# A two-layer decoder on one core: four chains with their own buffers, new engine orders, and the experts' weights applied on GpSimd

## The reference

```
g = silu(einsum('bsd,efd->bsef', x, Wg)); u = einsum('bsd,efd->bsef', x, Wu)
out_e = einsum('bsef,edf->bsed', g * u, Wd); routed_out = einsum('bsed,bse->bsd', out_e, w_full)
```

## Time and profile before

| | |
|---|---|
| executions of the kernel | 618.33 us median of 3 (615.70, 618.33, 619.99) |
| the profiled execution | span 616.0 us from first to last instruction |
| PE busy | 523.1 us (85% of the span), 2416 instructions |
| DVE busy | 498.5 us (81%), 1133 |
| ACT busy | 428.5 us (70%), 962 |
| POOL busy | 266.5 us (43%), 418 |
| DMA | 63.59 MB, mean 103 GB/s |

### The profile page before, as it was taken

One profiled execution on the slowest core, in us unless ns is written; L12 is line 12 of the kernel. 1 busy time (PEld: TensorE's weight loads), 2 busy tenths in 40 slices (PEclk: granted clock), 3 DMA queues, 4 the chain that ended last, 5 costly groups with the idle time before them and its releaser, 6 DMA issues.

```text
span 616.0 us, 8787 instructions
## 1 busy us (share of the span) xinstructions
PE 523.1 (85%) x2416; PEld 372.7 (60%) x2416; DVE 498.5 (81%) x1133; ACT 428.5 (70%) x962; POOL 266.5 (43%) x418
## 2 busy tenths in 40 slices
PE   4956674898776899999889998899999899989856
PEld 3534453566653567767566677676776767767634
DVE  2089999998989999999986979999899996544332
ACT  2597579699968867897966986995798692332211
POOL 1088567346785522647432565564344421101110
PEclk9876587699979999999989999899999999999969
DMA  7295020382204460166005550560272047042000
GB/s 201 79 377 201 1 70 1 101 264 87 69 1 112 127 194 2 50 196 197 0 1 151 144 147 5 167 202 1 77 232 64 2 129 235 0 129 94 10 0 9
DMA packets 29823, 63.59 MB, mean 103 GB/s; under 512 B 4752, under 2 KB 8592, under 8 KB 29392
## 3 DMA queue, kind: packets, MB, share of 16 engines
q1 hardware_dynamic: 29776, 63.04, 33.3%
HBM read 61.91 MB, written 1.11 MB: 102 GB/s over the span
## 4 chain that ended last, share of the span: by engine, by line
PE 42%; DVE 26%; ACT 15%; issue 10%; POOL 3%; SPq 2%; DMA 1%; DVEq 0%; POOLq 0%; ACTq 0%
PE work L610 24%; PE work L667 9%; DVE acc L1187 5%; DVE st L1171 5%; ACT dA L962 5%; PE work L586 3%; PE h_bank L586 3%; DVE m L1136 2%; ACT L962 2%; DVE wk L1140 2%; ACT L831 2%; DVE h_tok L1089 2%; POOL dbu L548 2%; DVE du L1105 2%; DVE bst L1014 2%
## 5 line engine op out<-in xcount | busy, mean ns | idle before, releaser
L548 POOL TENSOR_TENSOR dbu<-du,b_rows 128x512 f32<-128x512 f32 x128 | 163.1, 1275 | 82.1 <-DVE st L1171 60.6
L962 ACT ACTIVATE dA<-dts,a_neg 128x127 f32<-128x127 f32 x512 | 156.9, 355 | 17.2 <-DVE st L1171 16.1
L1171 DVE TENSOR_TENSOR_SCAN st<-dA,dbu 128x512 f32<-128x512 f32 x128 | 155.1, 1214 | 6.4 <-ACT dA L962 6.1
L586 PE MATMUL h_bank<-ident,st 128*128 128x128 f32 x512 | 89.1, 305 | 41.2 <-DVE acc L1187 32.4
L610 PE MATMUL work<-stream,xsT 128*128 128x352 f32 (+1 forms) x320 | 111.1, 485 | 4.5 <-ACT xsT L831 1.9
L586 PEld LDWEIGHTS h_bank<-ident,st 128*128 128x128 f32 x512 | 66.3, 156 | 74.3 <-DVE st L1171 55.6
L1187 DVE SCALAR_TENSOR_TENSOR acc<-h_bank,c_cols,acc 128x512 f32<-128x512 f32 x128 | 92.9, 726 | 0.5 <-PE h_bank L586 0.4
L610 PEld LDWEIGHTS work<-stream,xsT 128*128 128x128 f32 x320 | 59.4, 200 | 33.8 <-issue 3.6
L493 POOL TENSOR_SCALAR var<-mv 128x1 f32<-128x1 f32 x56 | 12.7, 227 | 132.0 <-DVE mv L1015 131.1
L831 ACT ACTIVATE h_t<-work 128x384 f32<-128x384 f32 (+2 forms) x64 | 30.8, 482 | 37.6 <-PE work L586 37.5
L962 ACT ACT_TABLE_LOAD x43 | 55.2, 1283 | 0.8
(11 more groups left out here) (159 smaller groups left out, 824.4 us busy)
## 6 DMA issues: line engine op xcount, KB each, us to landing
stream<-in_stream SPq DMA_DIRECT2D x72, 352.0 KB, 3.5
stream<-in_stream SPq DMA_DIRECT2D x32, 384.0 KB, 3.7
b_rows<-b_dram SPq DMA_DIRECT2D x32, 256.0 KB, 4.4
stream<-in_stream SPq DMA_DIRECT2D x8, 360.0 KB, 3.7
stream<-in_stream SPq DMA_DIRECT2D x8, 256.0 KB, 2.7
wg<-in_wg SPq DMA_DIRECT2D x1, 1280.0 KB, 8.5
wu<-in_wu SPq DMA_DIRECT2D x1, 1280.0 KB, 11.0
wd<-in_wd SPq DMA_DIRECT2D x1, 1280.0 KB, 13.6
```

What stands on the lines that cost most here:

```text
L548: gp.tensor_tensor(tile, du[:, batch % 2, :, lo:hi], b_rows[:, b % 2, k:k + 1, :].to_broadcast([P, ET, P]), ALU.mult).then_inc(s["dbu_read ...
L586: return nc.tensor.transpose(dst, src, ident[:, :])
L962: last = A(dA[i % DA_RING][:, t, 1:P], dts[:, batch % 2, t, lo + 1:hi], ACT.Exp, scale=a_neg[:, t, k:k + 1])
L1171: V.tensor_tensor_scan(st[:, i % ST_RING].rearrange("p t l -> p (t l)"), dA[i % DA_RING].rearrange("p t l -> p (t l)"), dbu[:, i % DBU_RIN ...
```

## The change

Six things are done together.

1. The chains `0` and `1` are cut in two each: `m` (out and xat0), `f` (ffn0), `h` (hgrn), `g` (ffn1). Each has its own `r`, `xsT`, `bst`, `mv`, `var`, `rstd` and semaphores; rows 2 and 5, which hand a unit from one chain to the next, are doubled. So the second chain of a layer can be at unit u while the first is at u + 1, or later.
2. All four orders and `BANK` are new.
3. SP has an order of its own, with letters for the loads (`l`), the chunks of the stream (`c`), the store and spread of B (`b`, `r`), rows of x (`w`, `x`) and the output rows (`o`).
4. `STREAM_RING` goes from 6 to 5 and `ACC_RING` from 4 to 3.
5. For a routed chunk, POOL multiplies the experts' weights into `h_tok` once ACT has written the SiLU there, one instruction for the chunk, with the weights broadcast along each expert's columns. DVE waits for that and makes one plain product of the chunk.
6. Some waits are new: a `D` sum waits for the normalised row of the unit before, `S` waits for its readers, and so on.

The diff, cut to its core (the new strings of `ORDER` and `BANK` are shortened to PE's last lines, the start of PE's and DVE's and that of SP's):

```diff
-ACC_RING = 4
+ACC_RING = 3
-STREAM_RING = 6
+STREAM_RING = 5
...
-    layer0 = [("out", k) for k in range(6)] + [("xat0", k) for k in range(5)] + [("ffn0", k) for k in F0.steps]
-    layer1 = [("hgrn", k) for k in range(8)] + [("ffn1", k) for k in F1.steps]
+    mixer0 = [("out", k) for k in range(6)] + [("xat0", k) for k in range(5)]
...
-        "0": [(stage, u, k) for u in range(U) for stage, k in layer0],
-        "1": [(stage, u, k) for u in range(U) for stage, k in layer1],
+        "m": [(stage, u, k) for u in range(U) for stage, k in mixer0],
+        "f": [("ffn0", u, k) for u in range(U) for k in F0.steps],
+        "h": [("hgrn", u, k) for u in range(U) for k in range(8)],
+        "g": [("ffn1", u, k) for u in range(U) for k in F1.steps],
...
     "pe": [
-        "ppp0ppppss00pppassssssaaaaaaaaaaaaasssssssssssss0ssp00sss00000spppssspsppsssss0000ss0ss0000s000000s0000s0s00s0",
+        "ppppppppmsmpassssssssssasssssssssssmmsmssssmmppssmspsspppsssffsmmmmpsssffffffffffppssspsfmmmmssffsfsfffsfmmsff",
...
-        "10100s110100001s1s111s1111011s000s00s0s111100000ss00001000000000001110100a110110000111111110000111000000000001",
-        "1110000001011110011111111111111111111111111111111111",
+        "gghsmmmmsffggfhhsfffgfsfggmmmfgmggffggmmggmgfffffffffffgfgfffgggfhhhhgghghfffffgfffhhffaaaaaaaaaaaaaffffffffgg",
+        "ffgfggghhhhghhgggghhgggggggggggggggggggggppsmmmfhhhg",
...
     "dve": [
-        "saa0000111pppppppsssssssssssssssspsppppppssassaaass0s00sssssas0s0as0ss00sp00s0ss00ppppppasa000aa000sa000000000",
+        "ppppppppsssssssssssssssssspsssssssmmmmmsmsssssmmsaaamsmsmasffsffspppppppafaffasasssassfffasasmmmmmsfffaamsfffs",
...
+    "sp": [
+        "lllclllcccbcrrlbccrccbxcwccccccccrccccccccrccccwcbcccwrcccccwcccccocccrccccccccoccccccccccccccccccccocrcwccccc",
+        "ccccccccccccocwccccocccccccccccccccccccccooo",
+    ],
...
-        row1, row2, row4, row5, row6 = (sb(f"row{i}", [P, H]) for i in (1, 2, 4, 5, 6))
-        row3 = sb("row3", [P, 2, H])
+        row1, row4, row6 = (sb(f"row{i}", [P, H]) for i in (1, 4, 6))
+        row2, row3, row5 = (sb(f"row{i}", [P, 2, H]) for i in (2, 3, 5))
...
-        r = [sb(f"r{i}", [P, H]) for i in range(2)]
-        xsT = [sb(f"xsT{i}", [P, HT, P]) for i in range(2)]
+        r = [sb(f"r{i}", [P, H]) for i in range(4)]
+        xsT = [sb(f"xsT{i}", [P, HT, P]) for i in range(4)]
...
+                if stage in ("ffn0", "ffn1") and isinstance(k, str) and k[0] == "U":
+                    f, c = (F0, F1)[stage == "ffn1"], int(k[1:])
+                    if f.lo[c] < f.routed:
+
+                        lo, hi = f.experts_of(c)
+                        pool.wait_ge(wf_ready[f.lay], b + 1)
+                        pool.wait_ge(*read(f"G{f.lay}_{c}", b))
+                        h = h_tok[f.lay][:, f.lo[c]:f.hi[c]].rearrange("p (e l) -> p e l", e=hi - lo)
+                        gp.tensor_tensor(h, h, wf[f.lay][:, lo:hi, :].to_broadcast([P, hi - lo, f.width]), ALU.mult)\
+                            .then_inc(weighed[f.lay], 1)
...
                 elif k == f.sum:
-                    add_bank(f.stage, u, rows(rows_in, u), lay)
+                    if u:
+                        dve.wait_ge(*row(rows_in + 1, u - 1))
+                    add_bank(f.stage, u, rows(rows_in, u), (FFN0, FFN1)[lay])
...
                     c = int(k[1:])
-                    dve.wait_ge(*read(f"G{lay}_{c}", u))
+                    if f.lo[c] < f.routed:
+                        dve.wait_ge(weighed[lay], f.routed_chunks * u + c + 1)
+                    else:
+                        dve.wait_ge(*read(f"G{lay}_{c}", u))
                     dve.wait_ge(*full(f"U{lay}_{c}", u))
                     t = work_bank(f"U{lay}_{c}", u)
-                    for lo, hi, e in f.weighted(c):
-                        h, up = h_tok[lay][:, lo:hi], t[:, lo - f.lo[c]:hi - f.lo[c]]
-                        if e is None and lay == 0:
-                            last = V.tensor_tensor(h, h, up, ALU.mult)
-                        else:
-                            weight = pr[:, 2:3] if e is None else wf[lay][:, e:e + 1]
-                            last = V.scalar_tensor_tensor(out=h, in0=h, scalar=weight, in1=up,
-                                                          op0=ALU.mult, op1=ALU.mult)
+                    h = h_tok[lay][:, f.lo[c]:f.hi[c]]
+                    up = t[:, 0:f.hi[c] - f.lo[c]]
+                    if f.lo[c] < f.routed or lay == 0:
+                        last = V.tensor_tensor(h, h, up, ALU.mult)
+                    else:
+                        last = V.scalar_tensor_tensor(out=h, in0=h, scalar=pr[:, 2:3], in1=up,
+                                                      op0=ALU.mult, op1=ALU.mult)
                     release(last, f"U{lay}_{c}", u)
```

More of the change, by code:

```diff
@@ L49, in __init__ @@
         self.chunks = len(self.lo)
+        self.routed_chunks = sum(a < self.routed for a in self.lo)
         self.k_tiles = -(-self.total // P)
@@ L86, in chains @@
         "a": [("adj", b, k) for b in range(B) for k in range(ADJ_STEPS)],
-        "0": [(stage, u, k) for u in range(U) for stage, k in layer0],
-        "1": [(stage, u, k) for u in range(U) for stage, k in layer1],
+        "m": [(stage, u, k) for u in range(U) for stage, k in mixer0],
+        "f": [("ffn0", u, k) for u in range(U) for k in F0.steps],
+        "h": [("hgrn", u, k) for u in range(U) for k in range(8)],
+        "g": [("ffn1", u, k) for u in range(U) for k in F1.steps],
+        "l": [("load", part, 0) for part in range(7)],
+        "b": [("store", b, 0) for b in range(B)],
+        "r": [("spread", u, 0) for u in range(U)],
+        "c": [("chunk", i, 0) for i in range(U * 3 * F0.chunks)],
+        "x": [("xT", b, 0) for b in range(3, B)],
+        "w": [("x", u, 0) for u in range(2, U)],
+        "o": [("rows", u, 0) for u in range(U)],
     }
@@ L168, in banks, with part_of @@
     return first + BANKS.get((stage, k), [])
-ROOTS0 = [("out", 4), ("xat0", 1), ("xat0", 3), ("ffn0", F0.sum)]
-ROOTS1 = [("hgrn", 4), ("hgrn", 5), ("hgrn", 6), ("ffn1", F1.sum)]
+MIX0, FFN0, MIX1, FFN1 = range(4)
+ROOTS = [[("out", 4), ("xat0", 1), ("xat0", 3)], [("ffn0", F0.sum)],
+         [("hgrn", 4), ("hgrn", 5), ("hgrn", 6)], [("ffn1", F1.sum)]]
+def part_of(stage):
+    return {"out": MIX0, "xat0": MIX0, "ffn0": FFN0, "hgrn": MIX1, "ffn1": FFN1}[stage]
 def decoder(nc, d, b_dram, out):
-    pe_order, dve_order, act_order, pool_order = (timeline(engine) for engine in ("pe", "dve", "act", "pool"))
+    pe_order, dve_order, act_order, pool_order, sp_order = (
+        timeline(engine) for engine in ("pe", "dve", "act", "pool", "sp"))
     with ExitStack() as ctx:
@@ L481, in _ @@
-            store_rows(U - 1)
+            for stage, i, k in sp_order:
+                if stage == "load":
+                    load_part(i)
+                if stage == "store":
+                    store_b(i)
+                if stage == "spread":
+                    spread_b(i)
+                if stage == "chunk":
+                    load_chunk(i)
+                if stage == "xT":
+                    sp.wait_ge(*full("gate", LT * (i - 2) - 1))
+                    sp.dma_start(xT[:, i % 3], d["xT"][:, :, i * L:(i + 1) * L]).then_inc(s["xT_loaded"], 16)
+                if stage == "x":
+                    sp.wait_ge(*row(1, i - 2))
+                    sp.dma_start(x_rows[:, i % 2], d["x"][:, i, :]).then_inc(x_loaded[i % 2], 16)
+                if stage == "rows":
+                    store_rows(i)
```

261 lines of the change are left out of this document (120 added, 141 removed).

## The result

The change makes the kernel faster by more than the range held: 571.7 us median of 5 (570.8 to 574.8) against 617.7 us of the kernel before on the same chip (5 runs); the ratio is 0.927, 95% interval 0.923 to 0.931. The forecast was 601.5 with a range of 586 to 619. The profiled span fell from 616.0 to 573.0 us. The profiled execution after is the slowest of its five (574.8 us; the spans of the others are 569.1 to 570.3), so the two traces show 3 us less than the medians do. In the runs recorded with both numbers an execution of the kernel before takes 2.1 to 2.6 us more than its span, one of the kernel after 1.8: that part is there each time and isn't scatter.

The account below looks back on a forecast made before the run. Bound: latency at the start, then DVE, then PE and DVE shared, then a tail of PE and latency. 616.0 - 4.0 - 9.0 - 11.6 + 3 + 15 - 8 - 2.3 = 599.1, plus 2.3: say 601.5 us, range 586 to 619.

Parts of the forecast that it names:

- DVE against POOL: DVE instructions between two SBUF tensors: longer as POOL's work grows by 19%, +3 us, bounds 0 and +22.
- Shared bound: After the fifth scan group up to the last scan step: PE at 94% gives back +15 us, bounds 0 and +25.
- Start: Up to the first scan: dt and bT come ahead of kv and the gate, -4.0 us, range -4.5 to 0.
- Products: Expert-weight products on DVE: 12.7 us less, of which -9.0 count ahead of the last scan step.
- Moved work: Four adjacency rounds and small DVE steps moved behind the last scan: -11.6 us, bounds -13 and 0.
- Loads: 20 fewer table loads on ACT, 25.7 us, a third counted: -8 us, bounds -25.7 and 0.
- Tail: Behind the last scan: hgrn of unit 7 spread between ffn1 steps of unit 6, -2.3 us, bounds -9 and +4.
- Rival (a): DVE stays the bound to the last scan and PE gives nothing back: 586 us, chance 0.14.
- Rival (c): POOL paces the scans, its weight operations waiting for late SiLUs with dbu behind: 633 us, by half 617; chance 0.14.

Follow-up runs that it names:

- b_pool_weights: The kernel before with the experts' weights applied on POOL and DVE's one product a chunk, in the old orders: 650.1 us, ratio 1.055.
- a_dve_weights: The kernel after with the experts' weights put back on DVE, one instruction per expert, none on POOL: 589.0 us, ratio 0.955.
- a_no_weights: The kernel after without any experts' weights, one DVE product a chunk behind the SiLU, none of them on POOL: 578.3 us, ratio 0.939.
- a_start: The kernel after with the old start: kv and gate ahead of dt, first five stream chunks behind all loads: 574.2 us, ratio 0.932.
- a_no_switch: The kernel after with plain copies in place of every SiLU and Tanh on ACT: 564.2 us, ratio 0.914.
- a_more_loads: The kernel after with ten one-element SiLUs in front of the scans' Exps, 16 more table loads: 587.0 us, ratio 0.951.

## Why the prediction was wrong

The sign was right and the size wrong: the span fell by 43.0 us, where the sum said 16.9 (in medians by 46.0). The 26.1 us between them lie in three places. By its own terms the prediction had the last sum at 510.8 - 14.6 = 496.2 and, 177 us earlier, the end of the fifth scan group at 319; it came at 304.7. That is 14.5 us, ahead of the shared stretch. The shared stretch took 168.9 us instead of 177: 8.1. The tail gave 5.8 instead of 2.3: 3.5. Two steps of the sum failed by what the traces measure, DVE against POOL and the shared bound; how the 14.5 us divide among the steps stays open. By its steps:

- **DVE against POOL, +3: wrong in sign, and the largest miss in an engine's work (20 us).** It said that DVE's instructions would take longer, since POOL has more to do. The same instructions took 17.6 us less, with POOL 14% busier. For the norms' last step alone it was 27.0 to 22.3 us; b_pool_weights has 29.2, a_dve_weights 23.8 with 42 us less on POOL than the kernel after. The loss goes with where POOL's operations fall, not with how many there are: of the instructions that are too long, 34 are left as 8. This fits the lock in the Trainium skill (SBUF — State Buffer, "SBUF: two separate sides"): all 34 overlap an operation of POOL, and 31 end within 0.3 us after it. With it the three terms for DVE's work ahead of the last sum, -9.0 - 11.6 + 3 = -17.6, stand against a measured -36.9. What those microseconds are worth in time is open. About 8 of the 17 lie ahead of the end of the fifth group, so they don't explain all of the 14.5 us there; a_no_weights, with 8 us of them back in all, is 7 us slower.
- **Shared bound, +15: mis-sized.** I took 94% as the pace that PE can hold. After the fifth scan group PE was busy 165.1 of 168.9 us up to DVE's last sum, 98%, with 166 us of work as forecast. The 94% was a trait of the old orders. (The sum itself is a little off too: 153 and 166 at 94% are 163 and 177, so +14.)
- **Start, -4.0: wrong.** `dt` began at 18.65, earlier as said, but 16 instructions took 6.80 us instead of 4.04, ACT put the gate's SiLU with its two loads ahead of the first Exp, and the first scan came 3.7 us later. It also didn't matter: the first group's last sum ends at 70.8 us, before at 69.6, and a_start, whose first scan starts 4.9 us earlier, is no faster.
- **Products, -9.0: the size was right, the worth not.** DVE's time fell by 12.9 us, at 0.51 and 0.68 us an instruction. In time they were worth some 10 us in the new orders, if the rest of a_dve_weights is collisions, and at most 4 in the old.
- **Moved work, -11.6: the worth isn't shown.** Four rounds did move behind the last scan. But 16 rounds less count 0 (before) and 3 us (after), so the place of four can hardly have been worth their 6.6 us.
- **Loads, -8: open.** 21 loads went. 16 loads more, with ten SiLUs, cost 15 us, but 65 less gave only 7.5 (a_no_switch), and before, 88 less gave 4. So the runs don't price the 21. There is no sign of the drain that the Trainium skill adds to each (ScalarE: Activation LUTs, "What ACT_TABLE_LOAD costs"): in a_more_loads 0.5 us of idle stand before 37 loads together.
- **Tail, -2.3: mechanism right.** Undone, it costs 12 to 13 us where I had 9.3 for the gap. The stretch behind the last sum's end, up to the last norm, shrank by 5.8 us (102.9 to 97.1).

Behind them is one error. I worked out what the old trace's bound would let go, engine by engine, with shares and losses of the old orders: a pace of 94% for PE, and collisions that grow with POOL's work. Both belonged to the old orders and changed with them. Rival (a), PE gives nothing back, was nearer (586), with a chance of 0.14; even it stopped 14 us short. That the sign came out right is no proof of the sum: the loads and the moved work may have been worth little, and what they lack was made up by terms that weren't in it. Rival (c) was real in part (late products and roots), but only in orders that aren't made for it.

## What to carry to other kernels

An engine that is busy 96% in a hand-ordered kernel needn't be the bound: take its work away in a run before pricing a change by it. In this kernel one removal under the old orders showed next to nothing and an addition showed nearly in full, so neither alone is the price of a part. Undoing a part exactly, in the new kernel, says what the new orders need it for, and not how the gain is made up. When the orders are made anew, don't carry over the shares of the old trace, neither an engine's pace nor what it loses to another engine. Look also at the longest durations of small instructions: where a median of 242 ns stands beside a longest of 779, the engine's busy time holds waiting.

## What the runs showed of the hardware

- POOL's product with the weights broadcast along the innermost axis is faster than one of two full tensors, where I had priced it by those: on average 778 ns at 352 columns and 1.06 us at 512, against 1.28 us for `dbu`. The 48 operations took 41.7 us, not 50.2.
- Some of DVE's instructions take longer beside POOL's, down to those on 8 numbers a partition (230 ns, with a longest of 779 before and 742 in a_no_weights). How much this costs depends on the orders: DVE has 34 instructions over 0.2 us too long in the kernel before, with POOL busy 266.5 us, and 8 in the kernel after, with POOL busy 304.6 us; without POOL's weight operations it has 20. With the weight operations on POOL DVE was busy 7.9 us less than without them.
- PE's clock at the start: with nothing ahead, the 16 instructions of `dt` and `bT` ran at a granted clock of 0.55, close to the level of 1.2 GHz, after 5.57 us of idle; behind the gate product, in a_start, the same ones ran at 1.00 (2.4 GHz). The granted clock of these stretches, after and then a_start:

```profile
18.65:25.45 6.80, 6.80 (x17) 3.74 (x17) 0.20 (x1) 1.92 (x3) 0.00 (x0) 0.55 0.39 152
```

```profile
20.04:23.80 3.76, 3.76 (x18) 2.22 (x16) 0.00 (x0) 2.40 (x4) 0.00 (x0) 1.00 0.00 0
```

  So the old gate product, which looked like an obstacle in the earlier trace rows, kept PE at work for what followed; moving it away won 1.4 us at the beginning of `dt` and lost 3.1 us in it, against a_start. (In the kernel before the gate product ran at 0.50 and `dt` and `bT` at 0.92, in 4.04 us.)
